# Graph network kernel, message pass: target numbers as rows in device memory, compared on VectorE

## The reference

```python
src, dst = (edge_index[0], edge_index[1])
x = jnp.concatenate([h[src], h[dst], edge_attr], axis=-1)
x = jax.nn.gelu(x @ mW1 + mb1)
x = jax.nn.gelu(x @ mW2 + mb2)
msgs = x @ mW3 + mb3
agg = jax.ops.segment_sum(msgs, dst, num_segments=h.shape[0])
count = jax.ops.segment_sum(jnp.ones((dst.shape[0], 1), dtype=h.dtype), dst, num_segments=h.shape[0])
agg = agg / (count + 1e-08)
```

## Time and profile before

| | |
|---|---|
| runs | 9023.61, 9052.6, 9022.56 us; median 9023.61 |
| profiled execution | span 9111.4 us from its first to its last instruction; the time around the span is not given |
| PE busy | 5811.4 us (64%) |
| DVE busy | 5087.2 us (56%) |
| POOL busy | 3666.3 us (40%) |
| ACT busy | 2786.5 us (31%) |
| message pass | 3496 to 5036 us of the span, 1540 us |

### The profile page before, as it was taken

How to read it: one execution, slowest core, us unless ns; L and a number is a source line. 1 busy time by engine, 2 the same in 40 slices (tenths; PEclk the granted TensorE clock), 3 DMA queues, 4 the chain that set the end, 5 groups by cost and what they waited for, 6 DMA issues and landing times. The chain is left out here.

```text
span 9111.4 us, 158678 instructions
## 1 busy us (share of the span) xinstructions
PE 5811.4 (64%) x46955; PEld 4772.3 (52%) x47287; DVE 5087.2 (56%) x12249; ACT 2786.5 (31%) x6113; POOL 3666.3 (40%) x3623
## 2 busy tenths in 40 slices
PE   2222226666577775888887357777773777777666
PEld 1111112665577673555555246666662666666566
DVE  7333433999678673333333556666665666666622
ACT  1000000578557552333333212222221222222210
POOL 2666661234000003555555245555551555555300
PEclk9999999887899897888888668788886878878788
DMA  4111113234324232334446033333352333333555
GB/s 158 43 41 43 42 43 138 77 126 135 112 99 155 100 108 80 116 112 115 119 113 109 11 83 96 92 95 94 94 91 46 95 93 92 94 93 94 66 183 188
DMA packets 662769, 884.50 MB, mean 97 GB/s; under 512 B 304425, under 2 KB 487254, under 8 KB 643668
## 3 DMA queue, kind: packets, MB, share of 16 engines
q1 hardware_dynamic: 553028, 674.48, 23.1%
q0 software_dynamic: 109568, 207.74, 11.5%
HBM read 648.77 MB, written 233.08 MB: 97 GB/s over the span
## 5 line engine op out<-in xcount | busy, mean ns | idle before, releaser
L979 POOL DMA_INDIRECT rows<-head_table,idxb x1760 | 1707.5, 970 | 1659.5 <-issue 474.9
L979 POOL DMA_INDIRECT rows<-source_table,idxb x880 | 842.7, 958 | 1808.6 <-ACT idxb L999 1156.7
L1692 DVE TENSOR_REDUCE gtop<-ps_top 128x1 f32<-128x512 f32 x1760 | 1208.2, 687 | 421.1 <-remote 248.1
L362 POOL DMA_INDIRECT records<-recb,idxb x784 | 773.4, 987 | 480.1 <-issue 451.2
L1829 PE MATMUL ps_top<-srow,sel 128*128 128x128 bf16 x7040 | 670.7, 252 | 298.3 <-DVE gtop L1692 240.4
L1829 PEld LDWEIGHTS ps_top<-srow,sel 128*128 128x128 bf16 x7040 | 551.3, 115 | 403.8 <-DVE gtop L1692 305.6
L1841 PE MATMUL ps_acc<-val,hot 128*128 128x132 f32 x3520 | 616.6, 325 | 89.5 <-issue 65.0
L777 PE MATMUL ps_cells<-hot 128*128 128x128 bf16 x4608 | 487.1, 250 | 251.4 <-DVE hot L735 105.7
L390 PE MATMUL ps_g<-hott 64*128 64x128 bf16 x784 | 100.9, 307 | 791.7 <-ACT hott L406 733.3
L1086 PE MATMUL ps_acc<-rows,pt 128*128 128x128 f32 x3750 | 516.5, 280 | 134.7 <-DVE pt L1107 120.8
L1841 PEld LDWEIGHTS ps_acc<-val,hot 128*128 128x128 f32 x3520 | 534.8, 227 | 125.0 <-issue 90.7
(11 more groups left out here) (328 smaller groups left out, 12775.8 us busy)
## 6 DMA issues: line engine op xcount, KB each, us to landing
logs<-log_counts SPq DMA_DIRECT2D x75, 1600.0 KB
hot<-one_hots SPq DMA_DIRECT2D x440, 256.0 KB
wt<-edge_weights SPq DMA_DIRECT2D x50, 1600.0 KB
one_hots<-hot SPq DMA_DIRECT2D x220, 256.0 KB
hott<-one_hots_t SPq DMA_DIRECT2D x440, 128.0 KB
edge_weights<-both SPq DMA_DIRECT2D x125, 320.0 KB, 2.6
log_counts<-none SPq DMA_DIRECT2D x125, 320.0 KB, 2.2
records<-blank SPq DMA_DIRECT2D x16, 1870.0 KB
```

The costliest lines, as they stand in the source:

```text
L362: g.indirect_dma_start(out=recs[:, :], out_offset=bass.IndirectOffsetOnAxis(ap=idxb[k][:, t:t + 1], axis=0), in_=recb[k][:, t, :], in_offs ...
L979: g.indirect_dma_start(out=rows[r][:, k, :], out_offset=None, in_=table, in_offset=bass.IndirectOffsetOnAxis(ap=idxb[r][:, k:k + 1], axis= ...
L1692: ve.tensor_reduce(gtop[:, h:h + 1], ps_top[h % TOPS][:, :], AX.X, ALU.max).then_inc(topped, 1)
```

## The change

The target numbers of the records are also kept in device memory as rows, in a new tensor `target_numbers` of 880 rows of 128 numbers in bf16, so that a group's 512 numbers lie in one stretch of 1 KB. `load_meta` makes them from `c.mt`, whose partitions are already columns: ACT copies each part to bf16 (in place of `c.dlob`) and SP stores it. In the message pass SP loads a group's row, `trow`, onto one partition, together with `feat` and on the same semaphore. PE spreads it over the partitions by one product with a row of ones. DVE compares the product in PSUM with the partition's own number and writes `hott`; ACT has no part in it any more.

```diff
@@ load_meta, SP @@
                     sp.dma_start(c.last[:, :], firsts[1:NB * CELLS + 1, :].rearrange("c a -> a c")).then_inc(last_in, 16)
+                    for n, rows in enumerate(parts):
+                        sp.wait_ge(rows_cut, n + 1)
+                        sp.dma_start(targets[n * P:n * P + rows, :], number_rows[0:rows, n, :]).then_inc(rows_stored, 16)
                     sp.wait_ge(last_in, 16)
+                    sp.wait_ge(rows_stored, 16 * len(parts))
@@ load_meta, ACT @@
-                        for m, to in enumerate((c.idx, c.dlo, c.wgt, c.dlob)):
+                        for m, to in enumerate((c.idx, c.dlo, c.wgt)):
                             cols = to[:, :, :].rearrange("p g k -> p (g k)")[:, n * P:n * P + rows]
-                            ins = act.activation(cols, ps_mt[:, m if m < 3 else 1, 0:rows], ACT.Copy)
+                            ins = act.activation(cols, ps_mt[:, m, 0:rows], ACT.Copy)
                         ins.then_inc(cols_out, 1)
+                        act.activation(number_rows[0:rows, n, :], c.mt[0:rows, n, 1, :], ACT.Copy).then_inc(rows_cut, 1)
@@ spread_targets @@
-def spread_targets(pe, c, ps, g):
-
-    for q in range(TG):
-        ins = pe.matmul(ps[0:BN, q * P:(q + 1) * P], c.dlob[:, bass.ds(g, 1), q].to_broadcast([P, BN]), c.identb[:, :],
-                        start=True, stop=True)
-    return ins
@@ mlp_pass, SP @@
                                      else rv[:, RING * i + r, :, 0:EF]).then_inc(feat_in[r], 16)
+                        sp.dma_start(trow[r][:, :], tv[bass.ds(RING * i + r, 1), :]).then_inc(feat_in[r], 16)
@@ mlp_pass, PE @@
-                            wait(pe, dist_ready, fg)
-                            spread_targets(pe, c, ps_tgt, fg).then_inc(tgt_ready, 1)
-                            pe.wait_ge(feat_in[r], (i + 1) * 16)
+                            pe.wait_ge(feat_in[r], (i + 1) * 32)
+                            wait(pe, hott_ready, fg)
+                            pe.matmul(ps_tgt[:, :], c.onesb[0:1, :], trow[r][:, :], start=True, stop=True).then_inc(tgt_ready, 1)
@@ mlp_pass, DVE @@
+                    ve.tensor_scalar(place[:, :], c.minus_p[0:BN, :], -1.0, None, ALU.mult).then_inc(place_set, 1)
+                    ve.wait_ge(place_set, 1)
...
                             one_hot(ve, c, hot[r], fg).then_inc(hot_ready, 1)
+                            ve.wait_ge(tgt_ready, fg + 1)
+                            wait(ve, sum1, fg - 3)
+                            wait(ve, hott_stored[r % 4], 16 * (2 * i + r // 4))
+                            ve.tensor_scalar(hott[r % 4][:, :], ps_tgt[:, :], place[:, 0:1], None, ALU.is_equal).then_inc(hott_ready, 1)
                             ve.wait_ge(featt_ready, fg + 1)
@@ mlp_pass, ACT @@
-                            act.wait_ge(tgt_ready, g + 1)
-                            wait(act, hott_ready, g)
-                            act.activation(dist[:, :], ps_tgt[0:BN, :], ACT.Abs, bias=c.minus_p[0:BN, :]).then_inc(dist_ready, 1)
-                            act.wait_ge(dist_ready, g + 1)
-                            wait(act, sum1, g - 3)
-                            wait(act, hott_stored[r % 4], 16 * (2 * i + r // 4))
-                            act.activation(hott[r % 4][:, :], dist[:, :], ACT.Relu, bias=c.ones[0:BN, 0:1], scale=-1.0) \
-                                .then_inc(hott_ready, 1)
```

30 lines of the change are left out of this document (16 added, 14 removed).

## The result

The changed kernel takes 9062.49 us (median of 19 runs, 9035.58 to 9078.88). On the same chip the kernel before takes 9032.13 us (19 runs, 9001.73 to 9061.46). The ratio is 1.0024 with a 95% interval of 1.0013 to 1.0035: slower by 0.24%, about 22 us. (The two medians are 30.4 us apart, 0.34%, which lies in the same interval.) I had forecast 9 us faster. The sign is wrong, and the time lies above the range. A little of the distance to my 9015 us is the base: I added to 9023.6 us, and the kernel before takes 8.5 us more beside the changed one.

The account below looks back on a forecast made before the run. It took a cycle with POOL's gathers to bound the message pass. Terms 0 (PE) - 10 (ACT) + 0 (DVE) + 0 (SP) + 1 (load_meta) = -9 us, from 9023.6 to 9015 us; own range 8990 to 9040, 8-in-10 range 8955 to 9055.

Parts of the forecast that it names:

- What bounds the kernel now.: Message pass: a cycle with POOL's gathers, 6.53 us a group, sets the pace; PE, DVE and ACT work has slack.
- the late signal: Message pass: PE's signal to POOL and `acc` comes at a fixed distance behind the gathers; `acc` starts about 1.2 us after.
- PE: four products and four weight loads out, one product in.: Target spread on PE: 0.22 us before and after; 0 taken, bounds -22 to +46 us over 220 groups.
- ACT: two instructions out.: Mask making on ACT: 1.40 us a group goes, mostly enlarging idle time; -10 us, a third of PE's 29.7 wait.
- DVE: one compare in.: Message pass, before the `featt` copy: 0.68 us a group, covered by DVE's idle time; 0 taken, bounds 0 and 150 us.
- The prediction's rule on the shared port: A compare reading PSUM is not in a two-port mode, so it doesn't keep GpSimd off the port; POOL cost 0.
- SP and the new transfer: Message pass: one more 1 KB DMA a group on SP; cost 0, or 90 us with cover gone.
- load_meta: Stage `load_meta`: seven 32 KB stores added and the last waited for; +1 us, between 0 and +3.
- A, the pass on ACT: Rival: the message pass hangs on ACT more than on POOL; 68 us won, 8956 us; chance 0.20.
- B, the compare paid: Rival: compare stretches DVE's row or the gathers; slower, 9174 us in full, 9099 in half the groups; chance 0.12.
- C, the late signal sooner with less posted: Rival: PE's late signal comes sooner with less posted by PE or ACT; 88 us won, 8936 us; chance 0.06.

Follow-up runs that it names:

- row half: Kernel before with the row, its transfer and the one one-row product, ACT's two mask steps kept (dist in bf16): ratio 1.0049.
- the product alone: Changed kernel without the row's transfer (1.0023, 9057.0 us) against the one with transfer and the four old products (0.9966, 9015.5 us), same chip.
- Alone, in four pieces: Changed kernel with the one-row product cut in four of 128 columns: 1.0009; the same four over 128 rows: 0.9986, both against the kernel before.
- One long piece of 128 rows: Changed kernel with its product over 128 rows, 127 of them zero: 1.0034 to the kernel before; 0.9995 on the 7768.29 us chip.
- compare half: Kernel before with ACT's two mask steps replaced by the DVE compare, four old products kept, no transfer: 0.9977, again 0.9966.
- The second compare: Changed kernel with the compare issued twice, the first into a tile nobody reads: 1.0048 to the kernel before.

## Why the prediction was wrong, point by point

- **What bounds the kernel now.** Right in kind. The pass hangs on the gathers and on PE signals behind them (two gathers a group: -4.5%), and POOL's pauses stayed: 1.82 us in the median of 152 between 3600 and 4900 us, against 1.89 of 168 before. Wrong in what I drew from it. I took the late signal to be the sum's, which only POOL and `acc` wait for, and so called PE's work slack. The same lateness also meets the signal of the second product, and then PE waits through `u` and the gelu. Before, that was already 121.3 us ahead of `u`, in a row that I did not read. The slack is there for more of the same work (an eighth of it came through), but not for this change.
- **PE: four products and four weight loads out, one product in.** This is the step that failed. I took 0 between -22 and +46 us, by the 0.22 us of 128-row products among their like. The row half measures +0.49% and +0.45%, 45 and 41 us, and the product alone 41.5 us, the upper end. That end was a product that takes 0.43 us, without its neighbours' overlap. What the trace shows is near that in size: two weight loads of about 0.1 us are exposed by the change from 128 rows to one and back, and the hold goes from 0.716 to 0.905 us, 42 us in 220 groups. The step from there to the time is not as simple. Alone, in four pieces, this costs 13 to 21 us. One long piece of 128 rows, without it, costs 48 us in its one measurement. Both together, in the change, cost 41 to 45. So the two don't add up, and how the price divides between them is open. In PE's own account it is the hold and slower products behind longer stops, and not more waiting in all.
- **ACT: two instructions out.** Sign right. The compare half wins 0.23% and 0.34%, 21 and 31 us, where I had 10. How much of that is PE's wait for the mask is less sure. Idle time ahead of the mask product reads 45.8 us before and 18.6 after, but my 45.8 and the bound drawn from it rest on missing records. Twice the 11.9 us of the groups with all three records is 24, so the fall is about 5 us. By the weight loads, which are all recorded, it is 18 (76.5 to 58.9). The row half, which keeps ACT's two steps, has 45.6 ahead of those loads, so this wait also falls without them. The rest of what the compare half wins has no row.
- **DVE: one compare in.** Right as far as it can be seen. It takes 750 ns in place of the 682 taken from the copy. The copy's idle time fell from 437.6 to 18.5 us, more than the 165 us of compare, because the compare now does that waiting (347.5 us). It was never priced alone, since it came with ACT's steps taken out. The second compare says what more of it costs, 22 to 32 us. The prediction's rule on the shared port held for this compare from PSUM: gathers stay at 947 ns in the median of the changed kernel (944 in the earlier trace rows).
- **SP and the new transfer; load_meta.** Right: nothing measurable. `load_meta` takes 102.1 us, against 103.1, where I had +1; that is within what its length varies between profiles (102.1 to 104.2).
- **Rivals.** A, the pass on ACT: no, the compare half wins at most 31 of its 68 us. B, the compare paid: its sign came true and its mechanism did not. C, the late signal sooner with less posted, and the time with it: no. With one product in place of four the sum's signal is late less often (70 of 169 seen against 117 of 177), as C had it, and the time goes up all the same. The second product's signal is late less often too, but longer when it is.

What stays open: why PE's signals come late beside four gathers a group on all chips used but one, and why one long product, or none, makes the second product's late signals longer where four short ones do not. The table shows a late `u` and a high ratio going together in twelve of thirteen rows. That is an association, not a mechanism. The 128-row piece, which gives PE's 0.19 us back, was 1.0034 where signals are late and 0.9995 where they are not. That would fit the lateness as a part of the price, and rests on one measurement of each.

The version that beats both is the compare with the four old products, 0.9977 and 0.9966 in two measurements, and 0.9966 a third time with the transfer left in. It needs neither the tensor of rows nor the transfer.

## What to carry to other kernels

A product whose weights have another number of rows than its neighbours' is not one product's time: count a weight load in the open on the way in and another on the way out, and see in the trace whether each load starts ahead of its product or together with it. Count the records of a line before reading its idle time: a missing first record looks like a wait. Test the halves of a change apart before arguing about it: here a gain of 0.2 to 0.3% and a loss of nearly 0.5% were sold as one. Where a signal comes late by microseconds, look who waits for each signal of that engine, and not only for the one that you noticed.

## What the runs showed of the hardware

- PE's signals can come long after the product: in the stretch shown, `u` starts over 5 us after its product ended. With two gathers a group, signals over 0.3 us late were seen only at the two ends of the pass. With four, 117 of 177 of the sum's were in the kernel before and 70 of 169 in the changed one, and on one chip none.
- That chip ran the same kernel in 7768.29 us, against 9032 to 9097 on the others, and only stages with gathers or scatters on POOL's queue were shorter: sorting of the records 1033.3 against 1264.5 us, the message pass 1192.6 against 1548.7, the later attention pass 2580.6 against 3327.4. All of these are the 128-row kernel on both chips. The stages between were within 1 us of each other (dense tiles 773.2 and 773.8, first attention pass 984.7 and 984.1). A gather takes 945 ns there too; what is missing in most groups is the pause behind the last one.
- The compare from PSUM took 750 ns for 512 elements, from bf16 in SBUF 354.
- Where the number of rows changes from one product to the next, the second one's weight load was not hidden under the first. With one product of one row in between, the first feature product starts 0.905 us after the first source-row product, with one of 128 rows 0.708.
